# The last expert layer in units of 128 rows, in parts of 8, 16 and 8 tiles

## The chip, the core and the metric

The kernel runs on one core of a Trainium2 chip. Its time is the device time of one launch in microseconds, and the number compared is the median of several runs. TensorE multiplies matrices (PE in the profile, PEld for its weight loads), VectorE is DVE, ScalarE is ACT, GpSimd is POOL, and SyncE is SP, which here only issues transfers.

## The reference

The model has four pairs of an attention layer and a feed-forward layer over 32 sequences of 128 tokens with 128 features (4096 tokens), each adding to x. Only the last pair matters here. Its attention has one head. Its feed-forward layer sends each token to the best 2 of 8 experts, with at most 1280 tokens for an expert:

```python
logits = x @ Wg.T
top_v, top_i = jax.lax.top_k(logits, K)
gates = jax.nn.softmax(top_v, axis=-1)
pos_f = ...                       # how many earlier tokens chose this expert
keep = pos_f < cap
exp_batches = zeros.at[flat_e, pos_safe].set(x[tok], mode='drop')
h = jnp.einsum('ecd,edf->ecf', exp_batches, W1)      # 128 -> 512
inp, gate = jnp.split(h, 2, axis=-1)
h = jax.nn.gelu(inp, approximate=False) * gate
exp_out = jnp.einsum('eci,eid->ecd', h, W2)          # 256 -> 128
out = segment_sum(gates * kept exp_out of each token)
```

## The kernel before

A stage of the program computes the last attention (`OneHeadFront`) and the expert layer (`capacity_ffn`) together. Each engine has its own list of work, written out by hand, and waits for the others by semaphores; within one engine nothing overtakes.

The attention runs over 8 groups of 4 sequences. The 32 tiles of 128 tokens are also cut into 4 chunks of 8 tiles, and chunks are routed as the attention frees them. Routing one chunk is, in order: `statistics` on DVE (L2426 and on), `inverse_root` on POOL (a power operation), `normalise` on DVE, `turn` and `logits` on PE with `copy_xn` on ACT between them, `choose` on DVE (best and second best expert), `count` on PE (how many earlier tokens chose each expert), `locate` on DVE (the row of each token in its expert's region), and then the scatter on POOL: 2 indirect transfers for each of 8 tiles, to `slots_in` in DRAM (L2400). From the second chunk of a loop on (`c >= 2`) a scatter is paced: before every second tile it waits until all scatters of its part so far have landed.

Chunks are grouped in parts, `CAPACITY_PARTS = [(0, 2), (2, 3), (3, 4)]`. A part is the unit in which results can start. When a part's chunks are located, DVE's `table` works out for each of the part's units which expert it belongs to and at which row it starts. A unit is 256 rows of one expert. The part has 16 units for its rows and 7 more for partly filled experts in part 0 (23), and 8 + 7 = 15 in parts 1 and 2: 53 units.

For a unit, SP's `load` reads the start row into a register and fetches the rows; the first load of a part waits for the part's table and for all of the part's scatters. PE transposes the rows (`turn_slots`), ACT copies them to SBUF (`copy_x`), DVE copies the expert's first weights to a fixed place (`copy_w1`, after reading the expert's number into a register), PE multiplies (`hidden`: 2 x 128 columns for Gelu in `h_bank`, 2 x 128 for the gate in `v_bank`), ACT evaluates Gelu, DVE multiplies the two (`gate_values`), PE multiplies by the second weights (`result`), ACT copies the result (`copy_y`), SP stores it to the part's `slots_out`. PE runs hidden of unit u+1 and the transposes of u+2 before result of u. DVE does `copy_w1(u + 3)` and `gate_values(u)` and, beside some units, `weigh`, pieces of `table`, `out_rows` and `add_result`.

When a part's units are all stored and its `out_rows` are known, POOL fetches for each of its tiles the two results of each token from `slots_out` (L2415), in a ring of 8 tiles, paced by two tiles in all parts but the last. DVE adds them, weighted, to x (`add_result`, two dependent operations), at the units that `added_beside` names, and SP writes x out in groups of 4 tiles. On POOL all scatters of all chunks stand before the first fetch.

In the kernel before, chunks 0 and 1 are routed beside the attention; chunks 2 and 3, the table of part 0 and the first weight copies follow it, and then come the units.

Of the kernel before, what the change touches and what calls it, by code (L numbers as in the profile page):

```python
# [16 lines left out]
S = 128  # L17
D = 128
TOK = NB * S
GB = 4  # L20
# [11 lines left out]
CAPACITY_PARTS = [(0, 2), (2, 3), (3, 4)]  # L32
# [2169 lines left out]
def capacity_ffn(nc, core, name, w1, w1_loaded, w2_dram, router_w, capacity, slots_in, slots_out, out, front):  # L2202
# [6 lines left out]
    UT = 256  # L2209
    unit_counts = [2 * (last - first) * CT // UT + NE - 1 for first, last in PARTS]  # L2210
    first_units = [sum(unit_counts[:p]) for p in range(len(PARTS) + 1)]
    NU = max(unit_counts)
    last_unit = first_units[-1]
    MOST = CT * max(last - first for first, last in PARTS) // UT
    ADDS = {0: 26, 1: 45}
    WBUF = 3
    BUF = 4
    XBUF = 6
    FORWARD = 5
# [5 lines left out]
    part_of_unit = [p for p, n in enumerate(unit_counts) for _ in range(n)]  # L2225
    ctx = ExitStack()
    with ctx:
# [23 lines left out]
        diff = [sb(f"diff{i}", [S, RT]) for i in range(2)]  # L2251
# [17 lines left out]
        expert_of = sb("expert_of", [S, last_unit], U32)  # L2269
        row_of = sb("row_of", [S, last_unit], U32)  # L2270
        xe = [sb(f"xe{i}", [S, 2, D]) for i in range(XBUF)]
        xT = [sb(f"xT{i}", [D, UT]) for i in range(3)]
        w1_u = [sb(f"w1_u{i}", [D, 2 * FC * 128]) for i in range(WBUF)]
        act_h = [sb(f"act_h{i}", [128, FC * UT]) for i in range(2)]
        h = [sb(f"h{i}", [128, FC, UT]) for i in range(2)]
        ye = [sb(f"ye{i}", [S, 2, D]) for i in range(BUF)]
        yg = [sb(f"yg{i}", [S, 2, D]) for i in range(RING)]
        t_bank = [pb(f"t_bank{i}") for i in range(2)]
        h_bank = [pb(f"h_bank{i}") for i in range(2)]
        v_bank = [pb(f"v_bank{i}") for i in range(2)]  # L2280
        y_bank = pb("y_bank")
        r_bank = pb("r_bank")
        WIDE = (RT + 1) * NE
        l_at = lambda c: (h_bank[0] if c < 2 else r_bank)[:, c % 2 * RT * NE:(c % 2 + 1) * RT * NE]
# [22 lines left out]
        w1_copied = sem("w1_copied")  # L2307
# [6 lines left out]
        y_stored = [sem(f"y_stored{i}") for i in range(BUF)]  # L2314
# [8 lines left out]
        def added_beside(b):  # L2323

            p = part_of_chunk[b // RT]
            return min(ADDS[p] + (b - PARTS[p][0] * RT) * 5 // 4, last_unit) if p in ADDS else last_unit

        @block.sync
        def _(sp):
            def load(u):  # L2330
# [7 lines left out]
                sp.dma_start(xe[u % XBUF][:, :, :], slots_in[bass.ds(at, UT), :].rearrange("(p j) d -> p j d", j=2))\  # L2338
                    .then_inc(x_loaded[u % XBUF], 16)

            def store(u):

                p = part_of_unit[u]
                sp.wait_ge(y_copied, u + 1)
                at = (u - first_units[p]) * UT
                sp.dma_start(slots_out[p][at:at + UT, :].rearrange("(p j) d -> p j d", j=2), ye[u % BUF][:, :, :])\
                    .then_inc(y_stored[u % BUF], 16)
# [11 lines left out]
            for u in range(FORWARD):  # L2359
                load(u)  # L2360
            for u in range(last_unit):
                if u + FORWARD < last_unit:
                    load(u + FORWARD)
                store(u)
# [9 lines left out]
        def _(pool):  # L2374
# [30 lines left out]
            for p, (first, last) in enumerate(PARTS):  # L2405
                pool.wait_ge(out_rows_done, p + 1)
                for i in range(BUF):
                    pool.wait_ge(y_stored[i], 16 * len(range(i, first_units[p + 1], BUF)))
# [10 lines left out]

        @block.vector  # L2420
        def _(dve):
            own = Steps(dve, dve_own)
            over_e = lambda v: v[:, :, None].to_broadcast([S, RT, NE])
# [685 lines left out]
```

## Time and profile before

| | |
|---|---|
| median of 3 runs | 1466.67 us (1466.66 to 1469.27) |
| span of the profiled execution | 1467.0 us |
| PE busy | 1171.7 us (80%) |
| DVE busy | 988.9 us (67%) |
| ACT busy | 667.1 us (45%) |
| POOL busy | 538.9 us (37%) |

The profile is of one execution, and its span agrees with the median to 0.3 us. The stage with the last attention begins at about 1173 us and the units of the last expert layer run from about 1282 to 1435. Times of rows are from the span's start. A wait is named by what ended it. The time of a transfer on POOL's queue (DMA_INDIRECT) is that of issuing it; it lands later.

### The profile page before, as it was taken

The page shows a single profiled execution, that of the slowest core. Times are in us where ns is not written, and L with a number is a line of the kernel's source. Part 1 is how long each engine was busy: PE and PEld are TensorE (multiplying, and loading weights), DVE is VectorE, ACT ScalarE, POOL GpSimd, SP SyncE. Part 2 cuts the span into 40 slices and gives each one's busy share as a digit, 9 for nine tenths or more (in the row PEclk, how much of TensorE's full clock was granted, in tenths as well). Part 3 has the DMA queues.
Part 4 walks back from the last instruction along what each step waited for, and adds up shares of the span by engine and source line. Part 5 has one row for each costly group of instructions (what it writes and reads, how often), then busy time and mean ns, then how long its engine had stood idle before and what let it go on. Part 6 is the DMA issues. An engine that isn't in the chain of part 4 may idle for free. (4 is left out here: it accounts for less than half of the span.)

```text
span 1467.0 us, 34935 instructions
## 1 busy us (share of the span) xinstructions
PE 1171.7 (80%) x11141; PEld 918.1 (63%) x11154; DVE 988.9 (67%) x2920; ACT 667.1 (45%) x1423; POOL 538.9 (37%) x590
## 2 busy tenths in 40 slices
PE   2699994439999957779987879999799956499991
PEld 1477773338899925556673456677477755399991
DVE  3689996474443347998984679888477777766552
ACT  1367762105555503345564546766234343144440
POOL 2324201664235256534411232431121125752554
PEclk9999997559999967899998989999799988599996
DMA  6887743012223258435532177564200042133542
GB/s 179 206 215 191 188 124 129 29 33 87 77 92 109 75 133 209 122 101 144 150 84 51 44 176 167 150 163 106 86 1 0 0 152 74 53 120 106 149 140 73
DMA packets 138978, 164.58 MB, mean 112 GB/s; under 512 B 15308, under 2 KB 118754, under 8 KB 131728
## 3 DMA queue, kind: packets, MB, share of 16 engines
q1 hardware_dynamic: 130664, 146.62, 37.0%
q0 software_dynamic: 8192, 16.46, 4.1%
q8 instruction: 60, 0.98, 0.3%
q14 instruction: 62, 0.51, 0.1%
HBM read 111.98 MB, written 51.38 MB: 111 GB/s over the span
## 5 line engine op out<-in xcount | busy, mean ns | idle before, releaser
L586 DVE TENSOR_REDUCE A_neg_max<-A_s_bank 128x4 f32<-128x512 f32 x384 | 253.2, 688 | 46.3 <-PE A_s_bank L725 35.9
L448 ACT ACTIVATE A_probsT<-A_st_bank 128x512 f32<-128x512 f32 x384 | 222.4, 602 | 40.4 <-PE A_st_bank L738 39.2
L725 PE MATMUL A_s_bank<-A_k_stack,A_q_stack 72*128 72x128 bf16 x1536 | 157.5, 228 | 38.0 <-DVE A_neg_max L586 22.3
L738 PE MATMUL A_st_bank<-A_q_stack,A_k_stack 128*128 128x128 bf16 x1536 | 153.1, 224 | 7.1 <-DVE A_q_stack L602 6.2
L738 PEld LDWEIGHTS A_st_bank<-A_q_stack,A_k_stack 128*128 128x128 bf16 x1536 | 112.5, 103 | 52.2 <-issue 42.9
L725 PEld LDWEIGHTS A_s_bank<-A_k_stack,A_q_stack 72*128 72x128 bf16 x1536 | 106.3, 102 | 52.1 <-DVE A_neg_max L586 33.4
L752 PE MATMUL A_pv_bank<-A_probsT,A_v_pad 128*32 128x128 f32 x3072 | 127.4, 284 | 1.5 <-issue 1.5
L2041 ACT ACTIVATE E_h<-E_h_bank,w_L_b 128x256 f32<-128x256 f32 x184 | 76.8, 471 | 72.4 <-PE E_h_bank L2141 71.0
L2153 PE MATMUL E_y_bank<-E_w,E_h 128*128 x736 | 90.3, 276 | 2.2 <-ACT E_h L2041 0.9
L752 PEld LDWEIGHTS A_pv_bank<-A_probsT,A_v_pad 128*32 128x32 f32 x3072 | 74.1, 111 | 24.7 <-issue 3.4
L2141 PE MATMUL E_h_bank<-E_xT,E_w_u 128*128 128x256 f32 x368 | 88.8, 386 | 0.0
L2153 PEld LDWEIGHTS E_y_bank<-E_w,E_h 128*128 128x128 f32 x736 | 86.0, 192 | 3.3 <-issue 3.2
L461 ACT COPY A_outT<-A_pv_bank 128x512 f32<-128x512 f32 x99 | 57.9, 585 | 64.7 <-PE A_pv_bank L752 64.6
L1715 POOL DMA_INDIRECT routed_in<-E_r,E_index x64 | 63.9, 999 | 62.0 <-DVE E_index L1845 35.3
L2415 POOL DMA_INDIRECT E_yg<-slots_out,E_index_out x64 | 61.5, 962 | 62.5 <-DMA slots_out<-E_ye 26.9
L310 POOL TENSOR_TENSOR A_split_r<-A_k_f,A_k_parts 128x512 f32<-128x512 f32 (+1 forms) x21 | 26.1, 1241 | 152.2 <-ACT A_k_parts L472 76.6
L2400 POOL DMA_INDIRECT slots_in<-E_xn,E_index x64 | 64.5, 1008 | 36.2 <-issue 16.5
L1916 DVE TENSOR_TENSOR E_ye<-E_y_bank,E_b 128x256 f32<-128x256 f32 x46 | 19.5, 425 | 84.3 <-PE E_y_bank L2153 84.2
L2141 PEld LDWEIGHTS E_h_bank<-E_xT,E_w_u 128*128 128x128 f32 x368 | 68.0, 195 | 7.7
L602 DVE COPY A_q_stack<-A_max_rows 32x2048 bf16<-32x2048 bf16 x96 | 69.8, 727 | 2.7
L767 PE MATMUL A_t_bank<-ident,A_outT 128*128 128x128 f32 x396 | 65.5, 289 | 4.8 <-ACT A_outT L461 4.8
L2563 DVE COPY E_w_u<-exp_w 128x512 f32 x53 | 23.0, 437 | 59.5 <-PE E_v_bank L2777 52.7
(371 smaller groups left out, 2641.4 us busy)
## 6 DMA issues: line engine op xcount, KB each, us to landing
A_q_stack<-q_scratch SPq DMA_DIRECT2D x48, 576.0 KB
A_k_stack<-k_scratch SPq DMA_DIRECT2D x32, 576.0 KB
q_scratch<-A_q_parts SPq DMA_DIRECT2D x48, 192.0 KB, 2.3
A_k_stack<-k_scratch SPq DMA_DIRECT2D x48, 192.0 KB
E_xe<-slots_in SPq DMA_DIRECT2D x53, 128.0 KB, 2.1
slots_out<-E_ye SPq DMA_DIRECT2D x53, 128.0 KB, 1.7
A_ctxT<-in_ctxT SPq DMA_DIRECT2D x24, 256.0 KB, 10.5
k_scratch<-A_k_parts SPq DMA_DIRECT2D x32, 192.0 KB
```

The lines of the kernel that those rows point to most:

```text
L448: act.activation(probsT[n % 2][:, c * HQ:(c + 1) * HQ, :], st_bank[c % 2][:, :].rearrange("k (a q) -> k a q", a=HQ), ACT.Exp, scale=scale) ...
L586: dve.tensor_reduce(neg_max[:, c * HQ:(c + 1) * HQ], s_bank[c % 2][:, :].rearrange("q (a k) -> q a k", a=HQ), AX.X, ALU.max, negate=True). ...
L602: dve.tensor_copy(q_stack[n // 2 % 4][MAX_ROWS, 0:BY_DVE, n % 2 * S:(n % 2 + 1) * S], max_rows[n % 2][MAX_ROWS, None, :].to_broadcast([2 * ...
L725: last = pe.matmul(s_bank[c % 2][:, a * S:(a + 1) * S], q_stack[slot][0:COMBO, h, at:at + S], k_stack[slot][0:COMBO, h, at:at + S], start= ...
L738: last = pe.matmul(dst, k_stack[slot][:, h, at:at + S], q_stack[slot][:, h, at:at + S], start=True, stop=spread)
L752: last = pe.matmul(pv_bank[a * VW:(a + 1) * VW, c * S:(c + 1) * S], v_pad[p][:, n % GB, h % vheads, :], probsT[n % 2][:, h, :], start=True ...
L767: last = pe.transpose(t_bank[:, a * S:(a + 1) * S], outT[:, a, :], core.ident[:, :])
L1715: pool.indirect_dma_start(out=slots_in[:, :], out_offset=bass.IndirectOffsetOnAxis(index[:, k, b:b + 1], 0), in_=r[:, b, :], in_offset=Non ...
L2041: last = act.activation(h[u % 2][:, f, :], h_bank[(2 * u + q) % HB][:, f % 2 * UT:(f % 2 + 1) * UT], ACT.Silu, bias=b1[:, bass.ds(e * FC + ...
L2141: last = pe.matmul(dst, w1_u[u % WBUF][:, f * 128:(f + 1) * 128], xT[u % 3][:, :], start=True, stop=True)
L2153: last = pe.matmul(y_bank[:, j * D:(j + 1) * D], h[u % 2][:, f, j * S:(j + 1) * S], w2[:, bass.ds(e * (FC * D) + f * D, D)], start=(f == 0 ...
L2400: pool.indirect_dma_start(out=slots_in[:, :], out_offset=bass.IndirectOffsetOnAxis(index[:, k, b:b + 1], 0), in_=xn[:, b, :], in_offset=No ...
```

## The change

Parts become chunks 0, 1 and 2 together, and 3: `[(0, 1), (1, 3), (3, 4)]`. A unit is 128 rows, so the parts have 23, 39 and 23 units, 85 in all. `turn_slots` is one transpose, `hidden` has half the columns for the same weights, `result` half the passes. Buffers: 4 of first weights, 3 for Gelu, product and `v_bank`, 4 of transposed rows, 12 of loaded rows, one `t_bank`. PE runs hidden of u+2 and the transpose of u+4 before result of u. Results are copied and stored in pairs of units. Expert numbers are packed, four to a word in octal digits, so each engine reads a register once in four units and takes the digit by a shift. With `W1_EVERY = 1` DVE copies the first weights of every unit (ACT would take part at 2).

Only chunks 0 and 1 and the table of part 0 are done beside the attention. The routing of chunks 2 and 3 is spread between units, and so are the Exp operations of all four chunks. POOL's order becomes scatter 0, 1, 2, fetch of part 0, scatter 3, fetch of part 1, fetch of part 2; the inverse root of chunk 2 stands at tile 4, that of chunk 3 at tile 16, and scatters are paced from chunk 1 on. SP's `load_beside` fetches up to 11 units ahead, and begins a new part 6 units before it.

```diff
-CAPACITY_PARTS = [(0, 2), (2, 3), (3, 4)]
+CAPACITY_PARTS = [(0, 1), (1, 3), (3, 4)]
+W1_EVERY = 1
...
-    UT = 256
+    UT = 128
...
-    ADDS = {0: 26, 1: 45}
-    WBUF = 3
-    BUF = 4
-    XBUF = 6
-    FORWARD = 5
+    PACK = 4
+    ADDS = {0: 46, 1: 69}
+    WBUF = 4
+    HBUF = 3
+    XTBUF = 4
+    XBUF = 12
+    FORWARD = 11
+    NEAR = 6
+    PAIRS = 3
...
+        def load_beside(u):
+            p = part_of_unit[u]
+            return max(u - FORWARD, first_units[p] - NEAR + (u - first_units[p]) // 2 if p else 0)
+
+        def expert(eng, u, held):
+            if in_word(u) == 0:
+                eng.wait_ge(table_done, part_of_unit[u] + 1)
+            if held.get("word") != word_of(u):
+                held["word"] = word_of(u)
+                held["value"] = eng.value_load(experts_of[0:1, word_of(u):word_of(u) + 1], ...)
+            return (held["value"] >> (3 * in_word(u))) & (NE - 1)
...
 (GpSimd)
-            for c in range(NR):
+            def scatter(c):
                 pool.wait_ge(index_done, c + 1)
                 for b in range(c * RT, (c + 1) * RT):
-                    if b in (RT, RT + 2):
-                        inverse_root(2 if b == RT else 3)
-                    if c >= 2 and sent[p] and b % PACE == 0:
+                    if b in (RT // 2, 2 * RT):
+                        inverse_root(2 if b < RT else 3)
+                    if c >= 1 and sent[p] and b % PACE == 0:
                         pool.wait_ge(scattered[p], 16 * sent[p])
...
+            scatter(0)
+            scatter(1)
+            scatter(2)
+            gather(0)
+            scatter(3)
+            gather(1)
+            gather(2)
...
 (VectorE, after the attention)
-            statistics(3)
-            normalise(2)
-            table(0)
-            normalise(3)
             for u in range(WBUF):
                 copy_w1(u)
-            weigh(0)
-            weigh(1)
-            choose(2)
-            choose(3)
-            locate(2)
-            locate(3)
+            normalise(4)
             for u in range(last_unit):
                 copy_w1(u + WBUF)
                 gate_values(u)
+                if u == 0:
+                    normalise(5)
+                if u in (6, 7):
+                    choose(2, (u - 6,))
+                if u == 11:
+                    locate(2)
+                if u in (12, 13, 14):
+                    table(1, (u - 12,))
+                if u == 15:
+                    statistics(3)
+                if u in (17, 18):
+                    weigh(u - 17)
+                if u == 20:
+                    out_rows(0)
+                if u in (24, 25):
+                    normalise(u - 18)
+                if u in (32, 33):
+                    choose(3, (u - 32,))
+                if u == 37:
+                    locate(3)
+                if u in (38, 40, 42):
+                    table(2, ((u - 38) // 2,))
+                if u in (52, 54):
+                    out_rows((u - 50) // 2)
...
 (ScalarE)
             for u in range(last_unit):
+                if u + 2 < last_unit:
+                    activate(u + 2)
+                if u + 4 < last_unit:
+                    copy_x(u + 4)
+                if ends_pair(u):
+                    copy_y(u)
+                if u in (13, 14, 15):
+                    exponent(u - 13)
+                if u == 40:
+                    exponent(3)
...
 (TensorE)
             for u in range(last_unit):
-                    hidden(u + 1)
-                    turn_slots(u + 2)
+                    hidden(u + 2)
+                    turn_slots(u + 4)
+                if u in (0, 2):
+                    turn(4 + u // 2)
+                if u == 4:
+                    logits(4)
+                    logits(5)
+                if u == 9:
+                    count(2)
+                if u in (26, 28):
+                    turn(6 + (u - 26) // 2)
+                if u == 30:
+                    logits(6)
+                    logits(7)
+                if u == 35:
+                    count(3)
                 result(u)
```

In the diff, `normalise` is by groups of 4 tiles in the new lines and by chunks of 8 in the old ones.

## Rows read from the trace of the kernel before

**Rows 1.** The chain that ended last: start us, us, what (x merged pieces).

```profile
...
1275.47 2.25 DMA slots_in<-E_xn,E_index
...
1282.66 1.71 PE E_h_bank L2777 x4
...
1288.98 0.86 PE E_h_bank L2777 x4
...
1290.93 0.89 PE E_y_bank L2790 x8
...
1435.88 1.70 DMA slots_out<-E_ye
...
```

**Rows 2.** Stretches: from:to, length, busy (count) of PE, PEld, DVE, ACT, POOL, clock, DMA.

```profile
...
1235.00:1250.00 15.00, 9.89 (x73) 8.79 (x71) 10.29 (x49) 5.19 (x21) 11.05 (x12) 0.77 0.22 69
...
1290.00:1350.00 60.00, 60.00 (x382) 54.61 (x381) 39.02 (x129) 28.52 (x64) 25.79 (x26) 1.00 0.36 118
...
```

**Rows 3.** Groups over the span: operation, names, count | busy us, mean ns | idle before.

```profile
...
L2563 DVE COPY E_w_u<-exp_w 128x512 f32 x53 | 23.0, 437 | 59.5 <-PE E_v_bank L2777 52.7 <-DVE E_index_out L2553 3.5 <-DVEq L2537 1.8
...
L2684 ACT COPY E_ye<-E_y_bank 128x256 f32<-128x256 f32 x53 | 19.7, 372 | 29.1 <-PE E_y_bank L2790 29.1
...
L1916 DVE TENSOR_TENSOR E_ye<-E_y_bank,E_b 128x256 f32<-128x256 f32 x46 | 19.5, 425 | 84.3 <-PE E_y_bank L2153 84.2
...
```

**Rows 4.** Timeline of PE at the first unit: start us, us, operation [idle before].

```profile
...
1280.88 0.69 PE L2763 MATMUL E_t_bank<-ident,E_xe 128*128 128x128 f32 x2 [3.78 <-DMA E_xe<-slots_in]
...
```

**Rows 5.** Timeline of SyncE: the first six loads of units.

```profile
...
1278.75 5.86 SPq L2338 DMA_DIRECT2D E_xe<-slots_in  x6
...
```

**Rows 6.** Timeline of POOL: inverse root, scatters (L2400), fetches (L2415).

```profile
...
1251.06 1.67 POOL L2382 TENSOR_TENSOR E_rstd<-E_rstd,minus_half 128x8 f32<-128x8 f32 x1
...
1264.25 1.99 POOL L2400 DMA_INDIRECT slots_in<-E_xn,E_index  x1 [0.30 <-issue]
...
1322.04 0.98 POOL L2400 DMA_INDIRECT slots_in<-E_xn,E_index  x1 [2.18 <-DMA slots_in<-E_xn,E_index]
...
1329.15 0.97 POOL L2400 DMA_INDIRECT slots_in<-E_xn,E_index  x1 [2.30 <-DMA slots_in<-E_xn,E_index]
...
1333.07 0.97 POOL L2400 DMA_INDIRECT slots_in<-E_xn,E_index  x1 [0.30 <-issue]
1354.51 0.99 POOL L2415 DMA_INDIRECT E_yg<-slots_out,E_index_out  x1 [20.47 <-DMA slots_out<-E_ye]
...
1406.66 0.95 POOL L2415 DMA_INDIRECT E_yg<-slots_out,E_index_out  x1 [0.30 <-issue]
...
1438.31 0.94 POOL L2415 DMA_INDIRECT E_yg<-slots_out,E_index_out  x1 [6.44 <-DMA slots_out<-E_ye]
...
```

**Rows 7.** Timeline of DVE: first operations of statistics, normalising, table, copies, choosing, placing.

```profile
...
1251.79 1.65 DVE L2428 BATCH_NORM_STATS2 E_stats<-x_sb 128x6 f32<-128x128 f32 x8
...
1254.14 2.11 DVE L2438 TENSOR_SCALAR E_xn<-x_sb,E_mv,E_rstd 128x128 f32<-128x128 f32 x8
1256.16 0.43 DVE L2505 TENSOR_SCALAR E_kept<-E_base 128x8 f32<-128x8 f32 x2
...
1262.24 2.14 DVE L2438 TENSOR_SCALAR E_xn<-x_sb,E_mv,E_rstd 128x128 f32<-128x128 f32 x8 [0.15 <-DVE E_terms L2535]
1264.30 1.09 DVE L2563 COPY E_w_u<-exp_w 128x512 f32 x3
...
1268.88 0.22 DVE L2451 TENSOR_REDUCE E_top<-E_r_bank 128x8 f32<-128x64 f32 x1 [1.67 <-PE E_r_bank L2712]
...
1272.55 0.23 DVE L2451 TENSOR_REDUCE E_top<-E_r_bank 128x8 f32<-128x64 f32 x1
...
1277.13 0.23 DVE L2471 TENSOR_TENSOR E_place<-E_r_bank,E_base 128x64 f32<-128x64 f32 x1 [0.86 <-PE E_r_bank L2722]
...
1279.02 0.22 DVE L2471 TENSOR_TENSOR E_place<-E_r_bank,E_base 128x64 f32<-128x64 f32 x1
...
```

**Rows 8.** Timeline of ACT at the first Gelu.

```profile
...
1283.09 1.28 ACT L2678 ACT_TABLE_LOAD   x1
...
```

More of the change, by code:

```diff
@@ L2358, in _ @@
             layer.sync(sp, between)
-            for u in range(FORWARD):
-                load(u)
+            loads = 0
             for u in range(last_unit):
-                if u + FORWARD < last_unit:
-                    load(u + FORWARD)
-                store(u)
+                while loads < last_unit and load_beside(loads) <= u:
+                    load(loads)
+                    loads += 1
+                if ends_pair(u):
+                    store(u)
                 for g in range(NG):
@@ L2404, in _, with gather @@
                         sent[p] += 1
-            for p, (first, last) in enumerate(PARTS):
+            def gather(p):
+                first, last = PARTS[p]
                 pool.wait_ge(out_rows_done, p + 1)
-                for i in range(BUF):
-                    pool.wait_ge(y_stored[i], 16 * len(range(i, first_units[p + 1], BUF)))
+                stored = pair_of[first_units[p + 1] - 1] + 1
+                for i in range(PAIRS):
+                    pool.wait_ge(y_stored[i], 16 * len(range(i, stored, PAIRS)))
                 for b in range(first * RT, last * RT):
@@ L2658, in between, with copy_w1 @@
                         copy_xn(at)
-                if g == 6:
-                    exponent(0)
-            layer.act(act, between)
-            for g in range(4, NG):
-                copy_xn(g)
-            for c in range(1, NR):
-                exponent(c)
+            def copy_w1(u):
+                e = expert(act, u, held_word)
+                if u >= WBUF:
+                    act.wait_ge(v_ready, u - WBUF + 1)
+                act.copy(w1_u[u % WBUF][:, :], w1[:, bass.ds(e * W1, W1)]).then_inc(w1_copied[u % 2], 1)
@@ L2785, in result @@
+                j = u - pairs[n][0]
+                e = expert(pe, u, held_word)
                 pe.wait_ge(h_done, u + 1)
-                if u >= 1:
-                    pe.wait_ge(y_copied, u)
-                for j in range(2):
-                    for f in range(FC):
-                        last = pe.matmul(y_bank[:, j * D:(j + 1) * D], h[p][:, f, j * S:(j + 1) * S],
-                                         w2[:, bass.ds(e * (FC * D) + f * D, D)], start=(f == 0), stop=(f == FC - 1))
+                if j == 0 and n >= 1:
+                    pe.wait_ge(y_copied, n)
@@ L2792, in result @@
+                for f in range(FC):
+                    last = pe.matmul(y_bank[:, j * D:(j + 1) * D], h[u % HBUF][:, f * UT:(f + 1) * UT],
+                                     w2[:, bass.ds(e * (FC * D) + f * D, D)], start=(f == 0), stop=(f == FC - 1))
                 last.then_inc(y_ready, 1)
-            turn_slots(0)
-            turn_slots(1)
+            layer.pe(pe, between)
+            for u in range(4):
+                turn_slots(u)
             hidden(0)
+            hidden(1)
             pe.wait_ge(w2_loaded, 16)
@@ L2837, in program @@
         slots_in = dram("slots_in", (8 * TOK, D), F32)
-        slots_out = [dram(f"slots_out{i}", ((last - first) * 8 * 256 + 7 * 256, D), F32)
+        slots_out = [dram(f"slots_out{i}", (((last - first) * 16 + 7) * 128, D), F32)
                      for i, (first, last) in enumerate(CAPACITY_PARTS)]
```

243 lines of the change are left out of this document (137 added, 106 removed).

## The prediction

> **What bounds the kernel now.** I read the chain that ended last first, then the stretches, then the timelines of single engines. In the last layer the chain changes hands three times. First GpSimd scatters the rows of chunks 0 and 1 to the expert regions; the last of these 32 transfers starts at 1275.47 and lands 2.25 us later, and only then may a unit be loaded [rows 1]. From 1282.66 TensorE runs the units end to end: a full-clock unit of 256 rows is 0.86 for each hidden half, 0.22 for the transposes (1290.93 less 1288.98 and two halves) and 0.89 for the result, 2.84 us [rows 1], with PE busy in all of 1290 to 1350 at a clock of 1.00 [rows 2]; 53 units end some 0.4 (a copy of 0.37 [rows 3]) before the last store is issued at 1435.88 [rows 1]. Then the last unit is stored and GpSimd fetches chunk 3's 16 results from 1438.31; fetching, adding and storing take 28.7 us to the span's end at 1467.0 [rows 1, 6]. So the first and third legs are GpSimd's, the middle one TensorE's. What the reader must see: GpSimd issues one transfer about every 1.28 us, and every later scatter or fetch takes its turn in one queue.
>
> **The units.** A pass of 128 columns costs 0.111 us (0.89/8), with a weight load for each [rows 1]. A new unit has 1 transpose, 4 + 4 hidden and 4 result passes: 13 x 0.111 = 1.447 us. 85 units are 123 us, against 53 x 2.84 = 150.5. That is the gain of the change, 27.5 us, if TensorE stays the bound. VectorE does per unit a weight copy (0.437) and a product of 128x256 (0.425 in the nearest row) [rows 3]; they overlap by a little, so 0.8 us when the engine is free, 1.0 behind a chain of small dependent operations. At most it is 1.25 (with the half microsecond that it now idles before a copy, though TensorE ends most of that). ScalarE: copies of 128x256 take 0.37 [rows 3]; three smaller operations per unit are under 1.1. SyncE: six loads took 5.86 [rows 5], 0.98 each, and half a store, 1.2 per unit. All are under 1.447, so between extras the units go at TensorE's pace. VectorE can run about 2.2 us ahead of the result that needs its product (the hidden passes of a unit end 3.0 us before its result); what an extra costs beyond that stalls TensorE. The rest of the change (other ring sizes, packed expert words, stores in pairs, a split normalising) is inside these sums and hidden by TensorE's 1.447; uncovered, 0.15 more per unit would be 6 us in units 19 to 61.
>
> **The start.** Part 0 is now chunk 0 alone. Its 16 scatters were issued before the inverse root of 1251.06 [rows 6]; with that root moved among them they land by about 1254. The table of part 0 moves ahead of the attention's last group of additions, which ended at 1251.79 and had taken some 1.4; the table takes 6.1 (1256.16 to 1262.24) [rows 7] and a little more with the packed words: it runs from 1250.4 to 1256.9, later than the scatters, and sets the start. From release to the first transpose is 3.16 (1277.72 to 1280.88) [rows 1, 4]; three further loads at 0.98 come before the first hidden: it starts at 1263.5 instead of 1282.5, 19 us earlier. Two units of hidden passes at half clock (1.71 for what takes 0.86 [rows 1]), then result 0 ends at 1268.8.
>
> **The first boundary, where I expect the loss.** Units 23 to 61 belong to part 1, chunks 1 and 2. Unit 23's load waits for all 32 scatters of that part. Chunk 2's scatter comes behind the inverse root of chunk 3 in GpSimd's order, and that root waits for statistics(3), which VectorE now does after unit 15's product. Going there: result 6 at 1268.8 + 6 x 1.447 + 2.3 (two turns and the logits, about 20 passes) = 1279.8, its product 2.2 earlier, 1277.6. Then VectorE is the bound: choosing 3.67 (1268.88 to 1272.55), placing 1.89 (1277.13 to 1279.02), table pieces about 1.55, 2.75 and 3.0 (6.1, on 39 units instead of 23, and two more operations), statistics 2.35 (1251.79 to 1254.14) [rows 7]. Choosing, in halves with unit 7 between them, is over at 1277.6 + 3.67 + 1.0 = 1282.3. Unit 8's product and result (1.45) and on TensorE unit 11's hidden passes, a transpose and the count (1.5) bring the placing to 1285.4 at the latest; then 1.89 + 7.3 + 2.35 and four units at 1.0 give 1301.1. The root takes 2.2 (1.67 of it in one row [rows 6]): 1303.3. Chunk 2's 16 scatters go in pairs of tiles, each waiting for the last pair to land: three times 7.1 (1322.04 to 1329.15) and 3.9 to the last start (1333.07) [rows 6], which lands 2.25 later: 1303.3 + 21.3 + 3.9 + 2.25 = 1330.7. SyncE sits at this wait and TensorE, in order, at unit 23's transpose (before unit 19's result) until 1330.7 + 3.16 = 1333.9. TensorE could have been there at about 1306: some 27 us of idling, the whole gain.
>
> **Part 1.** From there to unit 61's result: 0.45 + 42 x 1.447 = 61.2; half clock at the restart 2.0; chunk 3's turns, logits and count on TensorE 3.2; VectorE's extras beyond its lead 7.6 (choosing 0.7; placing and three table pieces 9.2 within six units, 3.9; eight additions, output rows and weights from unit 46, 3.0). Sum 74.0: 1407.9. The other way to the same place: unit 22's store leaves SyncE behind eleven loads, about 1345; fetching chunk 0 takes 25 (half of the 52.15 between 1354.51 and 1406.66, less a wait [rows 6]); chunk 3's scatter 25.2 and 2.25, load 3.16: unit 62's transpose at 1400.6, unit 61's result not before 1405.5. The two agree.
>
> **The tail.** Part 1 is now 16 tiles, and its fetch can't start before its last unit is stored: 0.4 for the copy and 2.43 from the store's issue to the fetch (1435.88 to 1438.31), then 52.15 for 16 tiles in pairs, then chunk 3's 28.7 [rows 1, 6]. Today only the last 28.7 stand behind the units, as the middle fetch runs beside them. Now 81 stand behind unit 61, and the 23 units of part 2 (33 us) hide under them. 1407.9 + 2.8 + 52.2 + 28.7 = 1491.6, and 1 for transfers that meet weight copies (next paragraph): span 1492.6. The profiled span is 1467.0 and the median of the runs 1466.67, so I forecast **1492 us**.
>
> **Two rules beside rows.** A scatter that began as three weight copies ran for 1.09 took 1.99 instead of 0.97 [rows 6, 7]. Copies go from 53 to 85, one per 1.45 us; of the 48 transfers on my path some 20 run beside units, three in ten of them meet a copy, and a meeting costs between nothing and a copy's 0.43 [rows 3]: 0 to 2.6, and I take 1. The Trainium skill (SBUF — State Buffer, "SBUF: two separate sides") says that GpSimd can't write descriptors while VectorE runs such an fp32 copy; the trace agrees, by 1.0 us in that scatter. By that rule every meeting would cost what is left of the copy, the upper end or 1494.
> The Exp of all four chunks moves between the Gelu evaluations, so tables change eight times at 1.28 (one row [rows 8]). Three pairs fall in units 13 to 15, whose followers wait for unit 23 anyway; the pair at unit 40 adds 2.8 to ScalarE within the lead: nothing. The Trainium skill (ScalarE: Activation LUTs, "What ACT_TABLE_LOAD costs") puts a switch at about 2.66 with a drain; by that the sum would be 1495. The row shows the load alone.
>
> **Rivals.**
> (1) Faster: unit 23 isn't held. Place: its transpose. It decides there if the last scatter of chunk 2 lands by about 1304, not 1331. For it: TensorE's saving is real and VectorE might reach unit 15 sooner. Then unit 61's result is at 1268.8 + 61 x 1.447 + 6 + 16 of VectorE's stalls = 1379, and with 83.7 the end is 1463. Against it: 16 units at TensorE's best pace alone put statistics(3) after 1290, and the 27 us of paced scatters follow.
> (2) The clock: where VectorE holds TensorE back, the clock may fall as in 1235 to 1250 (PE busy 66%, clock 0.77) [rows 2]. Over units 37 to 61 that is 25 x 1.447 x (1/0.77 - 1) = 11: 1503, or 1510 with a slower product, too.
> (3) The waits cost nothing: paced pairs land before the next pair is due (saving 2 each, 3 times in chunk 2, 7 times in the fetch) and VectorE's extras hide: 1492 - 20 - 6 = 1466, no change. Against it: the pairs of the trace waited in nearly all cases.
>
> **Chances.** Forecast (1478 to 1506) 0.65; clock 0.17; faster 0.12; no change 0.06. About 0.2%, 3 us, is what can be told from no change. Faster 0.12, same 0.06, slower 0.82. Range 1468 to 1518: below, statistics(3) 8 earlier, no stalls in part 1 and fewer waits; above, the clock case with VectorE at 1.25 per unit.
>
> **What would show it.** Right: TensorE idle for some 25 us before the first load of unit 23, SyncE waiting for scatters in it, the root between chunks 1 and 2 starting after unit 15's product, the fetch of chunk 1 beginning right after unit 61's store, and GpSimd without a gap from there to the end. Unit periods near 1.45 show the pass count right; 1.9 would mean that VectorE or ScalarE bounds all units. Wrong: a first load of part 1 before 1315, or a fetch of chunk 1 before 1390.

## The result, and the profile after

The changed kernel takes 1506.78 us (median of 4 runs, 1501.03 to 1508.71) against 1467.97 for the kernel before on the same chip (4 runs, 1466.66 to 1469.62). The ratio is 1.0233, with a 95% interval of 1.0205 to 1.0261: slower. The forecast was 1492 with a range of 1468 to 1518.

The profiled execution of the changed kernel is the 1501.03 one; its span is 1499.2. PE is busy for 1153.8 us (before 1171.7), DVE for 1000.2 (988.9), ACT for 676.1 (667.1), POOL for 537.0 (538.9). So TensorE is busy for 18 us less, and the execution is 32 us longer.

The timeline of PE, with the idle time before each operation in brackets:

```profile
...
1288.65 0.71 PE L2874 MATMUL E_y_bank<-E_w,E_h 128*128 x4 [0.78 <-DVE E_h L2623]
1291.80 0.71 PE L2874 MATMUL E_y_bank<-E_w,E_h 128*128 x4 [1.44 <-DVE E_h L2623]
1295.80 0.71 PE L2874 MATMUL E_y_bank<-E_w,E_h 128*128 x4 [2.21 <-DVE E_h L2623]
1299.36 0.71 PE L2874 MATMUL E_y_bank<-E_w,E_h 128*128 x4 [1.86 <-DVE E_h L2623]
1329.65 0.47 PE L2849 MATMUL E_t_bank<-ident,E_xe 128*128 128x128 f32 x1 [25.69 <-DMA E_xe<-slots_in]
...
```

The units started early, as meant. Then four results wait for VectorE's product, and after them comes the hole: unit 23's transpose waits 25.69 us for rows to be loaded. Before, TensorE had no gap in this stretch [rows 2]. What the load itself waited for stands in the timeline of POOL (scatters are L2435, fetches L2453):

```profile
...
1226.74 1.14 POOL L2435 DMA_INDIRECT slots_in<-E_xn,E_index  x1 [1.14 <-DVE E_index L2530]
...
1298.00 0.24 POOL L2415 TENSOR_SCALAR E_rstd<-E_mv 128x8 f32<-128x8 f32 x1 [21.43 <-DVE E_mv L2479]
...
1307.35 1.00 POOL L2435 DMA_INDIRECT slots_in<-E_xn,E_index  x1 [2.06 <-DMA slots_in<-E_xn,E_index]
...
1321.09 0.97 POOL L2435 DMA_INDIRECT slots_in<-E_xn,E_index  x1 [2.05 <-DMA slots_in<-E_xn,E_index]
...
1344.15 0.99 POOL L2453 DMA_INDIRECT E_yg<-slots_out,E_index_out  x1 [18.26 <-DMA slots_out<-E_ye]
...
1415.91 1.04 POOL L2453 DMA_INDIRECT E_yg<-slots_out,E_index_out  x1 [18.66 <-DMA slots_out<-E_ye]
...
1469.15 0.94 POOL L2453 DMA_INDIRECT E_yg<-slots_out,E_index_out  x1 [0.30 <-issue]
...
```

Read it from the top: GpSimd stands for 21.43 us at the inverse root, because VectorE finishes the statistics of chunk 3 only then. Chunk 2's scatter, which doesn't need that root, stands behind it, and three times its next pair of tiles waits 2.05 or 2.06 us for the last one to land. The fetch of part 1 starts at 1415.91; with the fetch of chunk 3 behind it, from 1469.15, GpSimd has no further gap but the pauses between pairs of tiles, and the end is at 1499.2. The rows that answer to [rows 6] are thus 1344.15, 1415.91 and 1469.15 for the three fetches, against 1354.51, 1406.66 and 1438.31.

The stretches of the trace (from:to, length, busy of PE, PEld, DVE, ACT and POOL with counts, clock, DMA share, GB/s) show where the units could not run, ran, and were over:

```profile
...
1303.00:1329.00 26.00, 0.96 (x9) 0.77 (x7) 4.06 (x14) 0.38 (x1) 13.63 (x14) 0.59 0.11 36
...
1337.00:1365.00 28.00, 27.99 (x252) 27.44 (x253) 19.46 (x71) 14.97 (x45) 11.86 (x12) 1.00 0.41 115
...
1416.00:1469.00 53.00, 26.14 (x207) 23.75 (x205) 20.52 (x58) 13.16 (x40) 30.53 (x32) 0.83 0.35 97
...
```

One step was not in the forecast. ScalarE copies unit 61's result early enough:

```profile
...
1407.09 0.27 ACT L2759 COPY E_ye<-E_y_bank 128x128 f32<-128x128 f32 x1 [0.29 <-PE E_y_bank L2874]
...
```

but the timeline of SyncE shows its store, the last row, only at 1413.36:

```profile
...
1399.25 1.49 SPq L2371 DMA_DIRECT2D E_xe<-slots_in  x2
1400.79 0.43 SPq L2379 DMA_DIRECT2D slots_out<-E_ye  x1
1401.99 4.22 SPq L2371 DMA_DIRECT2D E_xe<-slots_in  x4
1406.26 0.43 SPq L2379 DMA_DIRECT2D slots_out<-E_ye  x1
1407.47 1.45 SPq L2371 DMA_DIRECT2D E_xe<-slots_in  x2
1408.96 0.43 SPq L2384 DMA_DIRECT2D out_x<-x_sb  x1
1410.16 1.57 SPq L2371 DMA_DIRECT2D E_xe<-slots_in  x2
1411.77 0.44 SPq L2379 DMA_DIRECT2D slots_out<-E_ye  x1
1412.98 0.34 SPq L2371 DMA_DIRECT2D E_xe<-slots_in  x1
1413.36 0.43 SPq L2379 DMA_DIRECT2D slots_out<-E_ye  x1
...
```

SyncE had stood at part 2's first load for 5.4 us, until chunk 3's scatter had landed. In the view of SyncE's waits (us in total, times, longest):

```profile
...
SPq L2369 <- DMA slots_in<-E_xn,E_index: 5.4, 1, 5.4
...
```

From there it worked off its list in order, eleven loads at about 1.1 us each among the older stores, and the store on which the fetch waits came 6.0 us after the copy (1413.36 less 1407.36). `load_beside` puts these eleven loads beside units 56 to 61, two to a unit, and a unit takes 1.53 us here. Experiment 6 below shows that the list makes nearly all of the delay without the wait ahead of it.

### The profile page after: what moved, and what is told of

Read it like the earlier page. It is cut to its first block and busy times, and to the rows that moved or that the text cites. A ratio compares the mean times of both kernels' runs of the same rounds, so it can differ in the third digit from the quotient of the medians.

```text
span 1499.2 us, 35917 instructions
## 1 busy us (share of the span) xinstructions
PE 1153.8 (77%) x11305; PEld 906.6 (60%) x11305; DVE 1000.2 (67%) x2994; ACT 676.1 (45%) x1486; POOL 537.0 (36%) x590
## 5 line engine op out<-in xcount | busy, mean ns | idle before, releaser
L2154 PE MATMUL E_y_bank<-E_w,E_h 128*128 x736 | 90.3, 276 | 2.2 <-ACT E_h L2042 0.9
L2453 POOL DMA_INDIRECT E_yg<-slots_out,E_index_out x64 | 61.5, 960 | 74.7 <-DMA slots_out<-E_ye 36.9
L2616 DVE COPY E_w_u<-exp_w 128x512 f32 x85 | 36.6, 433 | 61.5 <-PE E_v_bank L2862 53.7
L2435 POOL DMA_INDIRECT slots_in<-E_xn,E_index x64 | 63.1, 985 | 37.7 <-DMA slots_in<-E_xn,E_index 20.4
L2874 PE MATMUL E_y_bank<-E_w,E_h 128*128 x340 | 58.2, 296 | 21.3 <-DVE E_h L2623 21.0
```

The lines of the kernel that those rows point to most:

```text
L2154: last = pe.matmul(y_bank[:, j * D:(j + 1) * D], h[u % 2][:, f, j * S:(j + 1) * S], w2[:, bass.ds(e * (FC * D) + f * D, D)], start=(f == 0 ...
L2435: pool.indirect_dma_start(out=slots_in[:, :], out_offset=bass.IndirectOffsetOnAxis(index[:, k, b:b + 1], 0), in_=xn[:, b, :], in_offset=No ...
L2453: pool.indirect_dma_start(out=yg[b % RING][:, k, :], out_offset=None, in_=slots_out[p][:, :], in_offset=bass.IndirectOffsetOnAxis(index_ou ...
L2874: last = pe.matmul(y_bank[:, j * D:(j + 1) * D], h[u % HBUF][:, f * UT:(f + 1) * UT], w2[:, bass.ds(e * (FC * D) + f * D, D)], start=(f == ...
```

## How the runs are compared

The layers ahead of this one are the same code in all kernels, yet they do not take the same time in every execution. So beside the medians I give a length: from the first scatter of the last layer (1226.74 in the rows above) to the end of the span. Each length is of one profiled execution; the ratio is that of medians to the kernel before, with its 95% interval.

| kernel | first scatter | span | length | ratio |
|---|---|---|---|---|
| before | 1229.0 | 1467.0 | 238.0 | |
| changed | 1226.7 | 1499.2 | 272.5 | 1.0233 (1.0205 to 1.0261) |
| 1: root moved | 1230.5 | 1488.6 | 258.1 | 1.0132 (1.0098 to 1.0166) |
| 2: loads moved | 1223.5 | 1489.4 | 265.9 | 1.0162 (1.0132 to 1.0192) |
| 3: half the copies | 1233.0 | 1503.0 | 270.0 | 1.0221 (1.0186 to 1.0256) |
| 4: units alone | 1240.1 | 1478.8 | 238.7 | 0.9985 (0.9965 to 1.0006) |
| 5: 1 and 2 | 1232.8 | 1483.6 | 250.8 | 1.0094 (1.0065 to 1.0123) |
| 6: no pairs | 1232.0 | 1482.7 | 250.7 | 1.0103 (1.0051 to 1.0156) |
| 7: 1, 2 and 6 | 1228.1 | 1461.1 | 233.0 | 0.9976 (0.9952 to 1.0001) |
| 8: units, no pairs | 1230.3 | 1456.8 | 226.5 | 0.9911 (0.9886 to 0.9936) |
| 9: no table change | 1233.0 | 1506.3 | 273.3 | 1.0243 (1.0219 to 1.0267) |
| 10: four parts | 1236.2 | 1472.7 | 236.5 | 0.9984 (0.9968 to 1.0000) |

The first scatter lies between 1223.5 and 1240.1. The changed kernel's profiled execution came early, at 1226.7. With the median start of these twelve, 1231.3, and 1.9 us around the span, a length of 272.5 makes 1505.7, near the median of 1506.78, and 238.0 makes 1471.2, where the kernel before had medians of 1468.0 to 1472.4 beside the other kernels. So the 5.8 us by which the median lies above the profiled execution fit the start of the layer. The starts of the runs without a trace are not known, so that is a fit and not shown.

The medians are a second measure. For nine of the eleven kernels below the first row, the length less 238.0 and the median less that of the kernel before beside it differ by at most 1.6 us. For the changed kernel they are 34.5 and 38.8, for experiment 2 they are 27.9 and 23.3. A difference of lengths of 2 us or less is therefore not told from nothing, and what experiment 2 saves is read from its rows.

## The experiments

**1. The root behind the scatter.** In GpSimd's list:

```diff
-                    if b in (RT // 2, 2 * RT):
-                        inverse_root(2 if b < RT else 3)
+                    if b == RT // 2:
+                        inverse_root(2)
...
             scatter(2)
+            inverse_root(3)
             gather(0)
```

> The changed kernel with one edit: GpSimd does the inverse root of chunk 3 behind the scatter of chunk 2 and not ahead of it. My theory (the idling at unit 23 is chunk 2's scatter waiting for that root, which waits for the statistics after unit 15): the scatter starts when chunk 2 is placed, at about 1284 instead of 1300.4, unit 23's transpose comes at about 1314 instead of 1329.65, the idle stretch there falls from 25.7 to about 10 us, and the span is 14 to 20 us under the 1499.2 of the changed kernel (1479 to 1485). Rival A (the gain is eaten further down, as GpSimd's fetch of chunk 0, the scatter of chunk 3 or VectorE's extras set unit 61): unit 23 comes 16 us earlier, the span falls by under 5. Rival B (the scatter waits for something else, so the root is no cause): unit 23 stays within 3 us of 1329.65.

The timeline of POOL and the row of PE at unit 23's transpose:

```profile
...
1290.52 1.14 POOL L2435 DMA_INDIRECT slots_in<-E_xn,E_index  x1 [11.26 <-DVE E_index L2531]
...
```

```profile
...
1320.12 0.47 PE L2850 MATMUL E_t_bank<-ident,E_xe 128*128 128x128 f32 x1 [10.01 <-DMA E_xe<-slots_in]
...
```

The scatter now waits for its own indices, not for the root. Counted from the first scatter it starts at 60.0 instead of 73.6, unit 23 comes at 89.6 instead of 102.9, and the length falls by 14.4. The root is the cause of more than half of the hole; 10 us of it stay. Rivals A and B are out.

**2. Unit 61's store ahead of all but four of the loads.** In the rule that says beside which unit a load is issued:

```diff
             p = part_of_unit[u]
+            if p == 2 and u >= first_units[2] + 4:
+                return max(u - FORWARD, first_units[2])
             return max(u - FORWARD, first_units[p] - NEAR + (u - first_units[p]) // 2 if p else 0)
```

> The changed kernel with one edit: of part 2's loads only the first four are issued before the store of unit 61, the other nineteen behind it. My theory (SyncE, released at 1398.6, issues twelve loads before that store, which is why it comes 6.0 us after the copy of the result): the store is issued within 1 us of the copy, the fetch of chunks 1 and 2 starts 2.5 to 3.5 us after result 61 instead of 8.9, and the span falls by about 6 us to 1493. Rival A (the fetch would have waited for the earlier stores to land, or the units of part 2 now come too late): the span falls by less than 2 us. Rival B: the loads collide with the fetch, which takes over 56 us instead of 53.2, and nothing is won.

The result was copied at 1404.95. SyncE, and then POOL:

```profile
...
1403.52 1.78 SPq L2381 DMA_DIRECT2D slots_out<-E_ye  x2
1406.06 5.91 SPq L2373 DMA_DIRECT2D E_xe<-slots_in  x6
...
```

```profile
...
1407.37 0.98 POOL L2455 DMA_INDIRECT E_yg<-slots_out,E_index_out  x1 [13.12 <-DMA slots_out<-E_ye]
...
```

The store (the second of the two in the first row) is out before the other loads, the fetch starts 2.4 us after the copy instead of 8.6, and the length falls by 6.6. The fetch takes 52.0 (the next one begins at 1459.33), so the loads beside it cost nothing.

**3. Fewer copies on VectorE.**

```diff
-W1_EVERY = 1
+W1_EVERY = 2
```

> The changed kernel with the constant that says which units' first weights VectorE copies set to 2, so that ScalarE copies those of every other unit. My theory (VectorE bounds only the burst of units 6 to 15 and short ones in part 1, about 0.33 us per copy freed): statistics of chunk 3 end 1 to 3 us before 1297.8, unit 61 comes 2 to 5 us earlier, and so does the span (1494 to 1497). Rival A (VectorE's copy of every unit's weights is the main loss): the span falls by 15 us or more. Rival B (ScalarE with 0.43 more for every second unit holds the units back, or its queue delays the activations): unit periods rise above 1.5 us and the span is up by 3 us or more.

From the first scatter, the statistics of chunk 3 end at 69.5 instead of 71.1, unit 23 comes at 101.3 instead of 102.9, and the length is 2.5 shorter. The ratio, 1.0221, can't be told from 1.0233, and 2.5 us is little more than lengths can tell. A gain of 15 (rival A) and a loss of 3 (rival B) are out; the copies are a small matter.

**4. The short units without the new parts.** The changed kernel with the parts, the routing ahead of the units and GpSimd's order of the kernel before (the additions are moved, too, to unit 50 and later):

```diff
-CAPACITY_PARTS = [(0, 1), (1, 3), (3, 4)]
+CAPACITY_PARTS = [(0, 2), (2, 3), (3, 4)]
...
             scatter(2)
+            scatter(3)
             gather(0)
-            scatter(3)
             gather(1)
```

> The changed kernel's 128-row units, weight copies, packed words and rings, but with the parts of the kernel before (16, 8 and 8 tiles), all four chunks routed before the units, and GpSimd's order as before (four scatters, then the fetches). My theory (the units themselves save, the parts and the routing between units lose): units from 1281 at 1.45 us each end near 1406, the fetch of 16 tiles runs from about 1342 to 1394, that of chunk 2 to 1420, the last one starts there and the span is about 1449 (1446 to 1456), 18 us under the 1467.0 of before. Rival A (the short units don't pay, VectorE with its adds and copies holds them at 1.7 us): units end near 1427, the span is about 1459. Rival B (the units themselves cause the loss): the span is 1467 or more.

My theory was half right: the parts, the routing between the units and the order lose the whole 34 us together, since without them the length is that of before. But the units alone win nothing either (rival B's number). The timeline of POOL says why:

```profile
...
1370.35 1.00 POOL L2453 DMA_INDIRECT E_yg<-slots_out,E_index_out  x1 [25.80 <-DMA slots_out<-E_ye]
...
1450.02 0.95 POOL L2453 DMA_INDIRECT E_yg<-slots_out,E_index_out  x1 [0.30 <-issue]
...
```

GpSimd waits until 1370.35 for part 0's units and from there to the end has no gap but its pauses, the longest 3.54 us, so its fetches are the bound: the first two take 79.7, the last one starts with no wait for the units. TensorE's last result is at 1433.26, 16 us before. It took 142.3 us from the first transpose, at 1291.64, for 85 units, against 154.6 for 53 before (1280.88 to 1435.5 [rows 1, 4]): 12 us won and not the 27.5 that the pass count promised. A unit at 1.53 instead of 1.447 is 7 of the missing 15.

Part of the wait until 1370.35 is again SyncE's list. The last result of part 0 is copied by 1364.21, and its store is issued only at 1367.80, behind loads of the next part (a row each of ScalarE and SyncE):

```profile
...
1363.94 0.27 ACT L2751 COPY E_ye<-E_y_bank 128x128 f32<-128x128 f32 x1 [0.29 <-PE E_y_bank L2860]
...
1367.80 0.43 SPq L2379 DMA_DIRECT2D slots_out<-E_ye  x1
...
```

**5. Both moves together.** The diffs of 1 and 2.

> The changed kernel with both edits of the first two experiments (root of chunk 3 behind chunk 2's scatter; nineteen of part 2's loads behind unit 61's store). Layers ahead of the last one start it up to 16 us apart between executions of the same code, so the length counts from the first scatter to the span's end: 238.0 before, 272.5 changed, 258.1 with the root moved, 265.9 with the loads moved. My theory (two separate waits on one path): the savings add up, 14.4 + 6.6 = 21, length 251 to 253. Rival (with unit 23 early, unit 61's store no longer finds a backlog, since the scatter of chunk 3 ends before the units get there): length 256 to 259, as with the root alone.

The length is 250.8: 21.7 saved, against 14.4 + 6.6. They add up, and are two separate waits on one path.

**6. No waiting for pairs.**

```diff
-    PACE = 2
+    PACE = 1000
```

> The changed kernel with one constant changed, so that GpSimd no longer waits for a pair of tiles to land before it issues the next pair. My theory (the pairs wait for landings that a queue would have overlapped, 2 us each, three times in the scatters of chunks 2 and 3 and seven times in the fetch of chunks 1 and 2): unit 23 comes 6 us earlier, the fetch of 16 tiles takes 41 instead of 53.2, and the length from the first scatter falls from 272.5 to 252 to 258. Rival (the transfers themselves are the limit, so they land no sooner; or the pause is what let the units' loads and stores through): unit 23 and the fetch gain under 2 us each and the length stays over 268, or units 24 to 61 get slower by 3 us or more.

PE at unit 23, and the two ends of part 1's fetch on POOL:

```profile
...
1329.03 0.47 PE L2849 MATMUL E_t_bank<-ident,E_xe 128*128 128x128 f32 x1 [20.45 <-DMA E_xe<-slots_in]
...
```

```profile
...
1412.51 0.98 POOL L2453 DMA_INDIRECT E_yg<-slots_out,E_index_out  x1 [28.59 <-DMA slots_out<-E_ye]
...
1452.73 0.94 POOL L2453 DMA_INDIRECT E_yg<-slots_out,E_index_out  x1 [0.30 <-issue]
...
```

Unit 23 comes 5.9 earlier from the first scatter, and the fetch takes 40.2 instead of 53.2. The length falls by 21.8, more than the 15 to 20 expected. The transfers were not the limit; the pauses were. The units beside them were no slower: from unit 38's result to unit 61's they take 41.4 us, against 42.6 in the changed kernel.

Here SyncE also finds chunk 3's scatter landed when it comes to part 2's first load (min, median and longest ns of the wait, its start), while unit 61's result is copied as before:

```profile
...
L2369 SPq EVENT_SEMAPHORE  x1: 28/28/28, 1392.2 to 1392.2; - x1
...
1404.45 0.27 ACT L2759 COPY E_ye<-E_y_bank 128x128 f32<-128x128 f32 x1 [0.29 <-PE E_y_bank L2874]
...
```

The wait is gone, and the fetch still starts 7.8 us after the copy (1412.51 less 1404.72; 8.6 in the changed kernel). So it is the loads ahead of the store that delay it, and hardly the scatter for which SyncE had waited.

**7. All three.**

> The changed kernel with all three edits: the root behind chunk 2's scatter, the late loads behind unit 61's store, no waiting for pairs. My theory: the three savings add up, 272.5 less 14.4, 6.6 and 15 to 20, length 232 to 238, about that of the kernel before (238.0). Rival (GpSimd's order binds as a whole: the fetch of chunk 0, the scatter of chunk 3 and unit 62's load follow each other, and what the early parts win is waited for later): length 243 or more.

The length is 233.0, 39.5 under the changed kernel's and within the theory's range (the single savings sum to 42.8). The ratio to before, 0.9976, can't be told from no change.

**8. The units of experiment 4 without pairs.** Its other edits: `load_beside` returns `max(u - FORWARD, 0)`, the output rows stand beside units 22, 26, 30 and 34, and the additions begin beside units 47 and 75.

```diff
-    PACE = 2
+    PACE = 1000
```

> The kernel of the fourth experiment (128-row units, the parts and the order of before; length 238.7) without waiting for pairs, with part 1's and part 2's loads eleven units ahead throughout, in place of two per unit from six units ahead, and with the output rows four units apart. In the fourth experiment GpSimd had no gap from the fetch of part 0 at 1370.3 to the end, and TensorE was done 20 us earlier, so GpSimd was the bound there. My theory: the fetch of part 0 starts 3 to 8 us earlier and takes 41 instead of 54.6, the last unit sets the end again and is done about 190 to 193 after the first scatter, and the length is 222 to 228, so 10 to 16 us under before. Rival (GpSimd wasn't the bound, or the transfers without pauses hold the units back): length over 233.

The first and last fetch on POOL:

```profile
...
1357.63 1.23 POOL L2453 DMA_INDIRECT E_yg<-slots_out,E_index_out  x1 [33.87 <-DMA slots_out<-E_ye]
...
1427.99 0.94 POOL L2453 DMA_INDIRECT E_yg<-slots_out,E_index_out  x1 [9.15 <-DMA slots_out<-E_ye]
...
```

The last fetch again waits for the last unit (9.15 us), so TensorE sets the end. The length is 226.5, as expected, and the kernel is 0.9% faster than the one before (0.9911, 0.9886 to 0.9936): the one version here that beats both. Part 0's fetch starts only 2.9 us earlier from the first scatter, just under the 3 to 8 that I expected. That much is due to the loads and not to the pauses: part 0's last result is no earlier than in experiment 4 (124.4 against 123.8 from the first scatter), but its store now follows the copy by 0.1 us instead of 3.6. The pauses are the larger part, as the first two fetches, 79.7 us in experiment 4, now leave GpSimd waiting for the last unit; the edits were not run one by one.

The pauses alone were not taken out of the kernel before. Its last fetch waited 6.44 us for the units and not for GpSimd [rows 6], so there the pauses were not what set the end.

**9. No change of tables.** The kernel leaves out the Exp, so its output is not the reference's:

```diff
-                act.activation(diff[c][:, :], diff[c][:, :], ACT.Exp)
+                act.activation(diff[c][:, :], diff[c][:, :], ACT.Gelu)
```

> The changed kernel with Gelu in place of Exp for the differences of the router's logits (its weights of the two experts are then other numbers), so that no activation table is changed between the units. My theory (the eight table loads are hidden: three pairs before a wait that is longer, one pair within the lead): unit 23's transpose stays within 1 us of 102.9 after the first scatter, and the length from there to the span's end within 1.5 of 272.5. Rival (a switch costs TensorE what the skill's drain adds, most of all around unit 40): 3 to 6 us shorter.

Unit 23 comes at 102.4 from the first scatter (102.9) and the length is 273.3 (272.5): the eight table loads cost the changed kernel nothing that can be seen. The changed kernel's trace has one visible wait for them, 1.10 us at 1372.41, behind the pair at unit 40. Without the loads that wait is gone, and TensorE waits for VectorE in its place, longer than before (0.38 us at result 43 of the changed kernel):

```profile
...
1381.06 0.71 PE L2874 MATMUL E_y_bank<-E_w,E_h 128*128 x4 [2.05 <-DVE E_h L2623]
...
```

**10. Four parts.** The constants and GpSimd's list; VectorE's pieces are moved as the expectation says:

```diff
-CAPACITY_PARTS = [(0, 1), (1, 3), (3, 4)]
+CAPACITY_PARTS = [(0, 1), (1, 2), (2, 3), (3, 4)]
...
+            inverse_root(3)
             scatter(2)
             gather(0)
             scatter(3)
             gather(1)
             gather(2)
+            gather(3)
```

> A version made from what the runs showed: 128-row units as in the changed kernel, the first part still chunk 0 alone, but four parts of 8 tiles; chunk 2 is placed by unit 14 and chunk 3's statistics come before that; GpSimd does the root ahead of chunk 2's scatter, does not wait for pairs, and takes its turns in the order scatter 0, 1, 2, fetch 0, scatter 3, fetch 1, 2, 3; loads eleven units ahead. Seven more units (92). My theory (a fetch of 8 tiles beside the units and one behind them, no unit waiting for a scatter): units run from 35 after the first scatter without a stop, 92 at 1.5 and 8 to 14 of VectorE's extras, end at 181 to 187; then 3 and 28.8, length 213 to 219, against 238.0 before and 226.5 in the eighth experiment. Rival (VectorE or GpSimd binds: the routing between the units, or a fetch that comes late and holds the additions): length over 224.

A miss: 236.5, and the rival holds. No unit waits for a scatter any more, but TensorE needs 173 us from its first transpose at 1266.59 to the last result, 1.88 per unit. Two of its waits in this stretch (us in total, times, longest):

```profile
...
PE E_y_bank L2880 <- DVE E_h L2625: 10.8, 9, 2.3
...
PE E_t_bank L2855 <- ACT E_xT L2750: 4.3, 4, 1.5
...
```

VectorE's work between the units (routing, and from unit 34 on additions) is in the way for 10.8 us, and the three pairs of table loads that were free in the changed kernel now cost some 4 (1.48, 1.46 and 0.93), as nothing longer hides them:

```profile
...
1303.69 0.30 PE L2855 MATMUL E_t_bank<-ident,E_xe 128*128 128x128 f32 x1 [1.48 <-ACT E_xT L2750]
...
1307.07 0.30 PE L2855 MATMUL E_t_bank<-ident,E_xe 128*128 128x128 f32 x1 [1.46 <-ACT E_xT L2750]
...
```

The rest is passes for the routing, the half clock at the start and slower units (next section); I have not split it further.

## Why the prediction was right, and where its sizes were off

The sign, the place and the chain were right. The median, 1506.78, lies within the range but 0.8 above the 1478 to 1506 to which the prediction gave 0.65, where the clock rival had put 1503 to 1510; the clock is not what brought it there. In lengths, the forecast was 263.6 (1492.6 less 1229.0) and the trace shows 272.5, 8.9 more. By the steps:

- **The start.** Forecast 1263.5 for the first hidden passes, measured 1260.69; 2.3 of the difference is the earlier start of the layer.
- **The first boundary.** Statistics of chunk 3 were to end at 1301.1 and ended at 1297.81, 1.0 off after the same 2.3. VectorE bounds results 13 to 16, as the waits of 0.78 to 2.21 show. The idle time at unit 23, forecast about 27, is 25.69. Its place in the layer, 102.9, is 2.0 earlier than forecast. Experiment 1 shows that the root's order is what holds the scatter.
- **Part 1.** Forecast 74.0 from unit 23's transpose, measured 77.4, +3.4. The unit at 1.447 was too small. From result 43 to result 54 TensorE waits for nothing, and eleven units take 16.84 us, 1.53 each:

```profile
...
1374.83 0.71 PE L2874 MATMUL E_y_bank<-E_w,E_h 128*128 x4 [0.38 <-DVE E_h L2623]
...
1391.67 0.61 PE L2874 MATMUL E_y_bank<-E_w,E_h 128*128 x4
...
```

  For the sum's 42 units that is 3.5. That it comes so near to the whole difference is luck, as other terms were off and cancel. VectorE's extras, 7.6 in the sum, cost 3.7. The table load at unit 40, nothing in the sum, made TensorE wait 1.1. The waits of TensorE from 1330 to 1407 (us in total, times, longest) and the stretch in which the clock fell:

```profile
...
PE E_y_bank L2874 <- DVE E_h L2623: 3.7, 3, 2.4
PE E_t_bank L2849 <- ACT E_xT L2744: 1.1, 1, 1.1
...
1393.00:1407.00 14.00, 11.59 (x87) 11.09 (x85) 10.61 (x37) 5.42 (x17) 3.33 (x4) 0.88 0.20 59
...
```

  The fall that the second rival named is there, apart from the restart, only behind the longest of these waits, 2.41 at 1395.69: at a granted clock of 0.88, 87 passes take 11.59 us instead of 10.2 at the pace of the rows above, 1.3 more. 3.5 - 3.9 + 1.1 + 1.3 is 2.0; the other 1.4 I have not split.

- **From unit 61 to its fetch.** This is the term that was mis-sized: 2.8 was taken from the kernel before [rows 1, 6], and it measured 8.9, +6.1. The prediction counted one load and half a store per unit on SyncE, 1.2 us, under TensorE's 1.447. At the end of a part the list has two loads per unit, eleven ahead of the store of unit 61, and SyncE falls behind. The prediction let unit 22's store stand behind eleven loads, and did not ask the same of unit 61's. Experiment 2 removes the delay and gets 6.6 back, and experiment 6 shows that the wait for chunk 3's scatter has little part in it.
- **The tail.** 53.2 and 30.05 against 52.15 and 28.7, +2.4, of which 1 was set aside for transfers that meet weight copies. In the page of the changed kernel the groups of fetches and scatters (count | busy us, mean ns of one | idle before) are:

```profile
...
L2453 POOL DMA_INDIRECT E_yg<-slots_out,E_index_out x64 | 61.5, 960 | 74.7 <-DMA slots_out<-E_ye 36.9
...
L2435 POOL DMA_INDIRECT slots_in<-E_xn,E_index x64 | 63.1, 985 | 37.7 <-DMA slots_in<-E_xn,E_index 20.4
...
```

  Undisturbed ones take 0.94 and 0.97, so all 128 lose 64 x 0.020 + 64 x 0.015 = 2.2 us. But the 32 fetches on the path were no slower than 32 fetches of the kernel before. Stretches with POOL's busy time in fetches alone, of the changed kernel and of the one before:

```profile
...
1415.90:1469.10 53.20, 30.62 (x32) 0.83 0.34 96
...
1354.50:1406.60 52.10, 30.99 (x32) 1.00 0.49 146
...
```

  So the 1 us set aside is not there, still less the 2.6 of the upper end. The fetch is 1.1 us longer by the time between its transfers (22.6 against 21.2), in which the pairs wait; the longest of these seven waits is

```profile
...
1430.57 0.97 POOL L2453 DMA_INDIRECT E_yg<-slots_out,E_index_out  x1 [3.02 <-DMA E_yg<-slots_out,E_index_out]
...
```

  The other 1.3 lies behind the last store, issued at 1491.15 (before: 1460.35): 8.0 us from there to the end against 6.7. What fills them is open.

-2.0 + 3.4 + 6.1 + 2.4 - 1.0 is the 8.9. One reading in the prediction is off, and nothing in the sum hangs on it: the row of the weight copies [rows 3] has 1.1 us of idling before each (59.5 over 53), not half a microsecond.

Of the rivals, the first (unit 23 isn't held) did not happen, and experiment 1 shows that even 13 us less at that place would not have saved the change, as it leaves a length of 258. The third, that paced pairs cost nothing in the end, was wrong: in the changed kernel every pair of chunks 2 and 3 and of the paced fetches waited, 1.7 to 3.5 us, and experiment 6 puts the price at 21.8 us in the changed kernel. The eight table loads are free, as forecast; the higher sum by the Trainium skill's figure (ScalarE: Activation LUTs, "What ACT_TABLE_LOAD costs") did not come, and experiment 9 agrees with the row of the load alone. But experiment 10 shows that three of the four pairs were free because of the hole, and experiment 9 that the fourth was free because VectorE would have held TensorE there anyway.

The gain of the units was over-estimated, which the forecast did not notice, since the gain was lost anyway: experiment 4 has 12 and not 27.5 us of it on TensorE, and none at the end, because GpSimd's paced fetches had become the bound. Experiment 8, without the pauses, ends 11.5 us under the kernel before.

## What to carry to other kernels

Where one engine works through a list in order, ask of each wait that a change moves or adds what stands behind it on that engine, and who needs those items; the root ahead of a scatter cost 14 us here and eleven loads ahead of a store 6. When a faster engine wins time, look for the engine that then has no gap to the end: its issue rate and its pauses are the next price. Here taking the pauses away saved 21.8 us in the changed kernel, and the short units beat the kernel before only without them. When the code ahead of the change moves the end by 16 us between executions, measure from a mark inside the stage.

## What the runs showed that I had not expected

Transfers issued without pauses kept their pitch, and the units beside them were no slower: 16 tiles in 40.2 us, 1.26 for each of 32 transfers, beside units and loads, against 53.2 with a pause of about 2 us after every second tile. Loads placed two to a unit filled SyncE's list at the end of a part in the changed kernel and in experiment 4, and held the one store that mattered by 6.0 and 3.6 us. And twelve executions with the same layers ahead reached the last layer at anything between 1223.5 and 1240.1 us.
